# Loading each image tile by two transfers of eight rows per partition instead of one of sixteen

## The reference: what is computed

```python
# tokens: sums over 16 x 16 patches, then 12 channels -> 192 features
pooled = x.reshape(Bb, Cc, n, K, n, K).sum(axis=(3, 5))
h = jnp.einsum('bcij,ce->bije', pooled, channel_weights).reshape(Bb, n * n, EMBED)
# attention: the first 64 tokens of an image are queries, the other 132 keys and values
h = h + attn(layernorm(h), proj_w, proj_b)
# feed-forward: 8 experts of which each token takes 2, and one shared expert
y = jnp.einsum('tei,edi,te->td', silu(h1) * h3, w2, cw)
h = h + y + silu(x2 @ sw1.T) * (x2 @ sw3.T) @ sw2.T
```

## Time and profile before

| | before |
|---|---|
| three runs, median | 1804.97 us |
| the profiled execution | 1808.01 us |
| its span, first to last instruction | 1806.2 us |
| TensorE busy | 1512.9 us, 84% |
| VectorE, ScalarE, GpSimd busy | 1171.1, 884.0 and 763.5 us |
| bytes moved by DMA | 440.13 MB, 244 GB/s over the span |
| packets on q10 and q1 | 20,552 and 106,950 |

### The profile page before, as it was taken

How to read it: one execution, slowest core, us unless ns; L and a number is a source line. 1 busy time by engine, 2 the same in 40 slices (tenths; PEclk the granted TensorE clock), 3 DMA queues, 4 the chain that set the end, 5 groups by cost and what they waited for, 6 DMA issues and landing times. The chain is left out here.

```text
span 1806.2 us, 29976 instructions
## 1 busy us (share of the span) xinstructions
PE 1512.9 (84%) x9094; PEld 1184.7 (66%) x9094; DVE 1171.1 (65%) x2060; ACT 884.0 (49%) x2809; POOL 763.5 (42%) x761
## 2 busy tenths in 40 slices
PE   1821698989899798988889797998889898999997
PEld 1201575877668675877668675777668775787686
DVE  5856686677767586667768486676767686355521
ACT  2323565556545465546545564556635554234411
POOL 4328244623374244613464243723464243733431
PEclk9855799999999899999999899999999999999999
DMA  9896886678777787678768787678858784223330
GB/s 332 356 364 272 293 299 254 242 294 296 256 245 279 254 296 256 241 276 291 270 217 299 253 268 269 241 277 297 291 207 291 277 303 143 72 64 109 92 88 24
DMA packets 127674, 440.13 MB, mean 244 GB/s; under 512 B 14221, under 2 KB 80930, under 8 KB 105998
## 3 DMA queue, kind: packets, MB, share of 16 engines
q10 hardware_dynamic: 20552, 249.04, 36.6%
q1 hardware_dynamic: 106950, 189.06, 31.9%
HBM read 413.86 MB, written 20.07 MB: 240 GB/s over the span
## 5 line engine op out<-in xcount | busy, mean ns | idle before, releaser
L749 POOL TENSOR_TENSOR ffn<-ffn 128x384 f32<-128x384 f32 (+2 forms) x448 | 512.4, 1148 | 898.9 <-ACT ffn L927 796.2
L1523 PE MATMUL bank<-W2T,ffn 128*128 128x192 f32 (+1 forms) x3600 | 702.0, 332 | 6.6 <-DVE stage L1261 2.9
L1523 PEld LDWEIGHTS bank<-W2T,ffn 128*128 128x128 f32 (+1 forms) x3600 | 601.7, 190 | 76.5 <-issue 17.3
L1280 DVE TENSOR_TENSOR ffn<-bank,ffn 128x384 f32<-128x384 f32 (+2 forms) x504 | 310.7, 618 | 380.4 <-POOL ffn L749 170.4
L974 DVE TENSOR_REDUCE pooled<-xt 128x3 f32<-128x768 f32 (+2 forms) x375 | 447.9, 1196 | 18.4 <-DMA xt<-in_x 17.7
L927 ACT ACTIVATE ffn<-bank 128x384 f32<-128x384 f32 (+2 forms) x504 | 272.3, 542 | 355.4 <-PE bank L1538 132.5
L798 ACT ACTIVATE xt<-xt 128x256 f32<-128x256 f32 x809 | 329.9, 413 | 113.0 <-DMA xt<-in_x 82.1
L1538 PE MATMUL bank<-X2T,Wx 126*128 126x384 bf16 (+2 forms) x720 | 203.1, 355 | 54.8 <-DVE ffn L1280 38.9
L798 ACT ACTIVATION_READ_ACCUMULATOR xt<-xt 128x1 f32 x809 | 157.9, 195 | 0.0
L1367 PE MATMUL bank<-x0h,WT0h 128*128 128x512 f32 x288 | 130.5, 453 | 6.0 <-DVE ffn L1280 6.0
L1538 PEld LDWEIGHTS bank<-X2T,Wx 126*128 126x128 bf16 x720 | 58.1, 99 | 111.4 <-DVE ffn L1280 52.7
(11 more groups left out here) (234 smaller groups left out, 1791.2 us busy)
## 6 DMA issues: line engine op xcount, KB each, us to landing
xt<-in_x ACTq DMA_DIRECT2D x135, 1792.0 KB, 8.3
xt<-in_x SPq DMA_DIRECT2D x33, 1792.0 KB, 9.5
ffn<-cw_rows SPq DMA_DIRECT2D x192, 256.0 KB, 4.7
ffn<-cw_rows SPq DMA_DIRECT2D x192, 192.0 KB, 7.5
out<-stage SPq DMA_DIRECT2D x192, 96.0 KB
ffn<-cw_rows SPq DMA_DIRECT2D x64, 224.0 KB, 3.3
h2q<-Msb SPq DMA_DIRECT2D x64, 54.0 KB
ffn<-in_L_ffn_w SPq DMA_DIRECT2D x2, 768.0 KB
```

What stands on the lines that cost most here:

```text
L749: nc.gpsimd.tensor_tensor(out=cwb[slot][:, 0:n], in0=silu[(g.par + step) % 2][:, 0:n], in1=cwb[slot][:, 0:n], op=ALU.mult).then_inc(scaled, 1)
L1280: v.tensor_tensor(out=h[step % HR][:, 0:n], in0=h_ps(g, step, 1)[:, 0:n], in1=(silu[p] if e == NE else cwb[(c * NE + e) % CW_RING])[:, 0:n ...
L1523: last = mm(o, h[step % HR][:, 128 * t:128 * t + m], W2T[:, e, :], start=(e == 0 and t % 2 == 0), stop=(e == NE), skip_group_check=True)
```

## The change

Every load of an image tile becomes two, the first for image rows 0 to 7 of each partition and the second for rows 8 to 15, issued one behind the other on the same queue, behind the same waits. Each adds 16 to the semaphore of the slot, and the value that consumers wait for is doubled, so both pieces must have landed before anyone reads. The number of bytes, the order of the loads and all other instructions stay. The function `x_rows` is replaced by `load_tile`, which is called in the three places where a tile was loaded.

```diff
+PIECES = 2
...
     def landed(self, t):
 
-        v = 16 * ((self.off * TILES + t) // SLOTS + 1)
-        return v if self.k is None else self.k * (16 * 2 * TILES // SLOTS) + v
+        v = 16 * PIECES * ((self.off * TILES + t) // SLOTS + 1)
+        return v if self.k is None else self.k * (16 * PIECES * 2 * TILES // SLOTS) + v
...
-        def x_rows(num, t):
+        def load_tile(eng, num, t, slot):
 
             k, i = t // HALF, t % HALF
-            return xv[num, i, 128 * k:128 * k + 128, :]
+            for p in range(PIECES):
+                at = slice(ROW // PIECES * p, ROW // PIECES * (p + 1))
+                eng.dma_start(xt[:, slot, at], xv[num, i, 128 * k:128 * k + 128, at]).then_inc(x_in[slot], 16)
...
             for t in range(SLOTS):
-                sp.dma_start(xt[:, t, :], x_rows(0, t)).then_inc(x_in[t], 16)
+                load_tile(sp, 0, t, t)
...
-                sp.dma_start(xt[:, slot, :], x_rows(g.num(), t)).then_inc(x_in[slot], 16)
+                load_tile(sp, g.num(), t, slot)
...
-                act.dma_start(xt[:, slot, :], x_rows(g.num(), t)).then_inc(x_in[slot], 16)
+                load_tile(act, g.num(), t, slot)
```

## The result

The changed kernel takes 1785.29 us (median of four runs, 1777.85 to 1787.74) against 1806.66 us of the kernel before beside it: a ratio of 0.988, with an interval of 0.984 to 0.991. The gain is 21 us. The forecast was 1799, a gain of 6: the direction was right, but the result lies outside the forecast's own 1793 to 1803 and at the very edge of the whole range of 1785 to 1813, and the size was off by more than three times. Two more measurements of the same kernel gave 0.985 and 0.985, 27 us. The profiled execution took 1777.85 us, 30 us less than the profiled one of before; it was the quickest of its four, so the traces show the pattern and the medians the size.

The account below looks back on a forecast made before the run. The prediction took the seams, where `cw_rows` loads wait beside image loads, to bound the kernel. Its terms, 2 + 0 + 1.5 + 0.5 - 10 = -6 us, gave 1799 us against the runs' median, own range 1793 to 1803, whole range 1785 to 1813.

Parts of the forecast that it names:

- What bounds the kernel: At the seams, first steps of each new group, GpSimd waits for `cw_rows` loads slowed by image loads; 48.2 us lost.
- the 48.2 us: Excess of the six group-to-group distances with image loads at their seams over the last distance, 195.3 us.
- Part 1: First group's 21 DMA-bound tiles: more packets lengthen each by 0.1 us; +2 us taken, ends 0 and 3.
- Part 2: Image loads: the second piece's 2.3 us outside the transfer stays hidden behind the first; 0, else 48 us in first group.
- Parts 3 and 4: ScalarE's 135 extra issues after the beginning, mostly covered, +1.5 us; image tiles landing later beside the other queue, +0.5 us.
- Part 5: Seams: half packets shorten `cw_rows` waits behind images; -10 us, from the four milder seams, little in the two worst.
- My upper end, 43% of 48.2: Seams: waits behind images fall to 0.57 of themselves, so at most 21 us come back.
- No change: Rival: backlog of small store packets holds all seams, part 5 gives 0 to 3 us; some 1806 us, chance 0.23.
- Slower by exposed issues: Rival: after each load, ScalarE's second issue, 0.344 us for each of 135, is exposed; 1815 us, chance 0.17.
- Much faster: Rival: engines turn transfer by transfer, so worst seams' stall goes too, full 21 us; 1788 us or less, chance 0.12.
- Its remark on the clock: Much faster rival, worst seams: TensorE's clock doesn't sag behind the stall; no separate size given.
- The signs to look for: 21,504 more packets, `cw_rows` landings below 14 us, GpSimd's 93 us wait down a third, distances nearer 195.3 us.

Follow-up runs that it names:

- e3: Kernel before, image tiles whole, with each two-image query store issued as two stores of one image: 1762.4 us, ratio 0.975.
- e4: The changed kernel with query stores also issued image by image: 1767.6 us, ratio 0.978 to the kernel before.
- g4: Kernel before with stores by image and one transfer a tile in packets of 7,168 B: 1765.9 us, ratio 0.976.
- g3: The change with four transfers a tile instead of two, packets of 3,584 B: 1806.4 us, ratio 0.999 to the kernel before.
- e2: The change with tiles cut by partitions (64 each) instead of image rows, packets of 14,336 B: 2323.3 us, ratio 1.285 to the kernel before.
- f1: Kernel before with only the four image loads ahead of each seam in packets of 7,168 B, one transfer each: 1796.5 us, ratio 0.995.
- e1: Kernel before with one transfer a tile, packets capped at 7,168 B: 1790.4 us, ratio 0.991.
- h3: The change with its cut moved, two transfers a tile in packets of 13,440 and 896 B: 1807.7 us, ratio 1.000 to the kernel before.

## Why the prediction was right and wrong

**What bounds the kernel** was right: the seams, and the loads of `cw_rows` in them. One row was misread. I took TensorE's 4.38 us at 804.68 as a stall of this kind. It is there with the stores out of the way too; the change, then e3:

```profile
794.73 0.50 PE L1541 MATMUL bank<-X2T,Wx 126*128 126x384 bf16 x2 [4.02 <-issue]
```

```profile
786.42 0.82 PE L1541 MATMUL bank<-X2T,Wx 126*128 126x384 bf16 x2 [4.37 <-issue]
```

There the loop over pairs of groups jumps back; in the trace of before the record of TensorE's sequencer has a compare-and-branch of 7.5 us at 797.0, and in those of all other kernels one of 6.6 to 9.6 us at this place. "issue" meant just this: it waited for nothing. e3's third distance is 202.0 us, its others 194.2 to 198.3, so about 7 of the 9.3 us that I counted for the third seam could not be had, and the 48.2 us were really 38.7 (the six distances of before less those of e3, 1220.3 - 1181.6).

**Part 1, transfer time, +2.** The price was right, its weight wrong. GpSimd's first addition of successive tiles, in the change and with four transfers:

```profile
57.08 0.73 POOL L663 TENSOR_TENSOR ffn<-xt 128x256 f32<-128x256 f32 x1 [2.36 <-DMA xt<-in_x]
...
61.47 0.73 POOL L663 TENSOR_TENSOR ffn<-xt 128x256 f32<-128x256 f32 x1 [2.38 <-DMA xt<-in_x]
...
65.83 0.73 POOL L663 TENSOR_TENSOR ffn<-xt 128x256 f32<-128x256 f32 x1 [2.35 <-DMA xt<-in_x]
```

```profile
57.04 0.73 POOL L663 TENSOR_TENSOR ffn<-xt 128x256 f32<-128x256 f32 x1 [2.51 <-DMA xt<-in_x]
...
61.55 0.73 POOL L663 TENSOR_TENSOR ffn<-xt 128x256 f32<-128x256 f32 x1 [2.51 <-DMA xt<-in_x]
```

4.38 us instead of 4.29, where 4.4 was forecast; with quarters 4.51, so 0.22 us for 24 more packets, 9 ns each, against my 13. The median image packet took 535 ns at 14,336 B, 272 at 7,168 B (forecast 275) and 140 at 3,584 B. Yet the first mark moved by only 0.4 us, not 1.9. Why the rest doesn't reach it was not tried.

**Part 2, fixed cost of a transfer, 0.** Right: had it come through, the first group would be 48 us longer, and its mark moved by 0.4 us. The Trainium skill's wish for 1 MiB or more (DMA: Bandwidth & Descriptors, Bandwidth) doesn't bind here, where transfers are queued back to back. Its fit of 2.0 us stands in the same page's section Anatomy of one DMA — SWDGE (gpsimd) path, for DMAs that GpSimd issues, which these are not.

**Parts 3 and 4, issuing and late landing, +2.** Right in size as far as the runs tell: e4 is 1.7 us above g4, and the three traces of the change lose 5.1, 10.6 and 7.8 us between the seams, where one transfer with half packets loses 9.6 and 0.1. The cover holds for one more issue and no longer for three (g3). The issue of over 4 us at 194 us stands once in all kernels but e2 and was not doubled; TensorE's stall behind it is 4.25 us in the change and was 4.27.

**Part 5, the seams, -10: the step that failed.** Its price of a turn was right: `cw_rows` loads that follow each other come 2 to 3 us apart, forecast 2.8. At the four milder seams the distances show 3.8 - 2.1 + 2.8 + 5.0 = 9.5 us for a forecast of 10.1, and matmul by matmul 10.8, though not seam by seam. What failed is the sentence that I expect little in the two worst seams: their distances gave 8.9 + 12.0 = 20.9 us (17.6 and 14.2 in the other two profiles of the change), the seams alone 24.9. So the term that I had at -10 was -35.7 in this trace. I had counted only what is queued ahead of the load at its issue and held that number fixed. But the same packets share turns with images in the 20 us before; with half packets more of them have gone by then, 179 left instead of 265 at the second seam, and f1, which halves only those loads, gains 10.6 us. A queue's backlog is itself a result of the turns, and a change of the turns must be applied from the moment the backlog starts. My upper end, 43% of 48.2, also took the stall as proportional to the turn; once the stores are through in time the stall is nearly gone, not 43% smaller.

**The rivals.** No change: its condition, stores that hold the seams, was true, and its conclusion false, for the same reason. Slower by exposed issues: not at two transfers, but it is what the waits show at four. Much faster: its 1788 us was nearest to the result, though its sum was off (2 x 2.1 us in each of two seams and 10.1 elsewhere are 18.5, not 21). Its remark on the clock came true, and its mechanism falls. If an engine turned only after a transfer, e1 (16 half pieces on an engine in place of 8 whole ones, the same time a turn) would have gained nothing; it gained 16 to 18 us, and h3, with a second transfer, gained nothing.

The Trainium skill, in the section I had weighed (Queues, rings and completion order), has a turn of a packet of some 9 to 17 descriptors. The times alone don't exclude that, since a packet of nine would be halved by e1 as well. The packet records do. On one DMA engine, ahead of the second seam of before, each packet starts as the one in front of it ends: a store packet at 577.26 us, an image packet of 14,336 B at 577.29, a store packet at 577.83, an image packet at 577.86, a store packet at 578.43, an image packet at 578.46. Here an engine turns after each single piece.

**The signs to look for.** Packets: 39,992 + 111,702 - 127,502 = 24,192 more, 21,504 for images and 2,688 of semaphores, which I left out. GpSimd's wait for `cw_rows` was to fall by a third; in the first profile of the change it rose:

```profile
POOL ffn L752 <- ACT ffn L930: 746.6, 299, 12.4
...
POOL ffn L752 <- DMA ffn<-cw_rows: 115.3, 37, 11.7
```

It was 93.1 us in 17 times, and is 101.8 and 78.6 us, in 32 times each, in the other two profiles. One long wait per seam became one of 5 us and several of 2, for loads that now come one by one, while the wait for ScalarE fell by 50 us (30 and 3 in the others). The sum of an engine's waits for one cause was the wrong sign, since GpSimd is no bottleneck; the distances of the marks were the right one. And the sentence on where the prediction would be most wrong, a seam that changes its kind, was the right warning.

## What to carry to other kernels

Look at the outermost dimension of every store that shares a queue with loads somebody waits for: here 2 instead of 64 put the 96 KB of each store on two engines and cost 46 us of 1808, of which splitting the images gave back only half by a detour. Where small packets and large ones share DMA engines packet by packet, the size of the large ones sets the pace of the small ones, also for the backlog that builds up ahead of the moment you look at. Two causes for one stall call for an experiment that removes each by itself; if one edit alone beats both together, as here, the other was only treating the symptom.

## What the hardware showed that I had not expected

- A transfer to 64 partitions moves an image row of 14,336 B in about 1.06 us instead of 0.54 to 0.61, with the DMA engines 99% busy (e2).
- SyncE stands up to 10.7 us in the issue of a store of 96 KB when its queue is full on two engines; with e3 the longest of a query store is 1.2 us. The first row is of before; the second is of e3 and has its query stores alone.

```profile
L526 SPq DMA_DIRECT2D out<-stage x200: 511/599/10684, 233.9 to 1797.0; - x100
```

```profile
L524 SPq DMA_DIRECT2D out<-stage x128: 466/568/1228, 367.2 to 1757.8; - x128
```

- A loop's jump back cost TensorE's sequencer 6.6 to 9.6 us, 7.5 in the trace of before, while the compare that leaves the loop took 0.1 us. In TensorE's timeline it shows only as idle time of 4 us with "issue" behind it.
- Two queues on one DMA engine alternate packet by packet: a store packet of 768 B every 0.57 to 0.60 us beside whole image packets (before, 577.26 to 578.43 us).
